# Fifteen pair sums in place of twelve ahead of the transposes of a convolution, with new places for everything around them

## What is computed

```python
enh = _conv(_conv(x, w_conv1_pw, b_conv1_pw, 0), w_conv1_dw, b_conv1_dw, 1, groups=DIM)
h = _conv(x, w_conv2_g, b_conv2_g, 1, groups=INTERC)
h1, h2 = jnp.split(h, 2, axis=1)
attn = _conv(h1 * h2, w_conv2_pw, b_conv2_pw, 0) * attgamma + _conv(x, w_conv211, b_conv211, 0)
# _kba: each pixel has its own 3 x 3 kernel for a pair of channels, a mix of 16 learned sets by attn
bias = jnp.einsum('bpn,nc->bpc', att2, selfb[0])
attk = jnp.einsum('bpn,nm->bpm', att2, selfw[0])
y = jnp.einsum('bpgij,bpgj->bpgi', attk, uf).reshape(Bb, P, C) + bias
x2 = _kba(enh, attn, selfb, selfw) * ga1 + enh
return x2 + x
```

## Time and profile before

| | us |
|---|---|
| median of 3 runs (5731.08 to 5740.74) | 5735.58 |
| profiled execution, its own time | 5731.75 |
| its span | 5730.0 |
| busy TensorE, matmuls / weight loads | 5581.3 (97%) / 4131.5 (72%) |
| busy VectorE | 5083.3 (89%) |
| busy ScalarE | 3463.1 (60%) |
| busy GpSimd | 4185.7 (73%) |
| transposes of terms (L888), by each of the two identities | 6144 matmuls, 920 |
| products (L1100), to the ring / back to PSUM | 1792 of 1.22 / 512 of 1.23 |
| VectorE merges (L1106) | 512 of 1.22 |
| GpSimd merges (L811) | 256 of 2.39 |

### The profile page before, as it was taken

The page is one execution under the profiler, slowest core; times in us unless marked ns, Lnnn a source line. Parts: engine busy times, 40 slices in busy tenths (PEclk is TensorE's granted clock), DMA queues, the critical chain, the costliest instruction groups (busy, mean ns, idle before and its releaser), DMA issues.

```text
span 5730.0 us, 115887 instructions
## 1 busy us (share of the span) xinstructions
PE 5581.3 (97%) x39944; PEld 4131.5 (72%) x39944; DVE 5083.3 (89%) x5319; ACT 3463.1 (60%) x4284; POOL 4185.7 (73%) x1831
## 2 busy tenths in 40 slices
PE   8999999999998699999999999999999999999998
PEld 7888888888886366666666766666666666766666
DVE  7888888888887789999899998989999899998989
ACT  6888888888886455455554555555455554555553
POOL 4565555555654678888888888888888888888885
PEclk9999999999999799999999999999999999999999
DMA  2222222222221222222222222222222222222221
GB/s 89 73 73 73 73 73 77 77 73 73 73 73 62 52 72 67 69 64 65 73 67 70 62 65 71 67 71 66 68 64 65 73 67 70 62 65 71 67 71 45
DMA packets 155248, 394.20 MB, mean 69 GB/s; under 512 B 35136, under 2 KB 38400, under 8 KB 155136
## 3 DMA queue, kind: packets, MB, share of 16 engines
q1 hardware_dynamic: 154800, 392.87, 22.0%
q10 hardware_dynamic: 400, 0.69, 0.1%
HBM read 219.37 MB, written 136.31 MB: 62 GB/s over the span
## 4 chain that ended last, share of the span: by engine, by line
PE 54%; DMA 8%; DVE 3%; SPq 1%; issue 1%; ACT 1%; DVEq 0%; POOLq 0%; POOL 0%; ACTq 0%
PE ps_t L888 18%; PE ps_k L871 17%; DMA xin<-layer_out 8%; PE ps_m L854 8%; PE ps_p L840 5%; PE ps_t L905 2%; DVE products L1100 2%; PE ps_t L896 1%; PE ps_t L903 1%; PE ps_m L861 1%; ACT out_sb L991 1%; SPq L736 1%; DVE products L1062 0%; SPq L684 0%; SPq L711 0%
## 5 line engine op out<-in xcount | busy, mean ns | idle before, releaser
L805 POOL TENSOR_TENSOR enh<-enh,tap 128x1280 f32<-128x1280 f32 (+1 forms) x1024 | 2512.9, 2454 | 485.2 <-ACT tap L1009 431.7
L1100 DVE TENSOR_TENSOR products<-ps_k,enh 128x1024 f32<-128x1024 f32 x1792 | 2157.4, 1221 | 269.4 <-PE ps_k L871 248.5
L871 PE MATMUL ps_k<-att,basis 128*128 128x512 f32 x4608 | 1719.3, 459 | 22.1 <-DVE products L1100 10.9
L1009 ACT ACTIVATE tap<-e,dw 128x1280 f32<-128x1280 f32 (+1 forms) x1024 | 1260.6, 1251 | 0.0
L871 PEld LDWEIGHTS ps_k<-att,basis 128*128 128x128 f32 x4608 | 719.4, 190 | 701.2 <-DVE products L1100 451.1
L296 POOL TENSOR_TENSOR hidden_lo<-hidden,hidden_hi 128x1024 fp32r<-128x1024 f32 x256 | 693.1, 2726 | 717.2 <-DVE hidden_hi L501 717.2
L888 PE MATMUL ps_t<-ident_swap,products 128*128 128x128 f32 x6144 | 921.7, 273 | 0.0
L888 PE MATMUL ps_t<-ident,products 128*128 128x128 f32 x6144 | 919.7, 272 | 0.2 <-POOL products L811 0.2
L888 PEld LDWEIGHTS ps_t<-ident,products 128*128 128x128 f32 x6144 | 757.3, 140 | 175.7 <-POOL products L811 0.5
L811 POOL TENSOR_TENSOR products<-products 128x1024 f32<-128x1024 f32 x256 | 611.8, 2390 | 268.0 <-DVE products L1100 268.0
L888 PEld LDWEIGHTS ps_t<-ident_swap,products 128*128 128x128 f32 x6144 | 719.9, 141 | 0.0
(11 more groups left out here) (111 smaller groups left out, 7378.1 us busy)
## 6 DMA issues: line engine op xcount, KB each, us to landing
xin<-layer_out SPq DMA_DIRECT2D x64, 1280.0 KB, 7.2
xt<-in_x SPq DMA_DIRECT2D x128, 512.0 KB, 4.0
layer_out<-xo SPq DMA_DIRECT2D x128, 512.0 KB, 2.9
x_own<-layer_out SPq DMA_DIRECT2D x128, 512.0 KB, 4.0
out<-out_sb SPq DMA_DIRECT2D x256, 256.0 KB, 2.0
att<-att_hi SPq DMA_DIRECT2D x512, 32.0 KB, 1.9
att<-att_lo SPq DMA_DIRECT2D x512, 32.0 KB, 2.0
h_up<-h_sb SPq DMA_DIRECT2D x256, 16.0 KB
```

The lines of the kernel that those rows point to most:

```text
L805: nc.gpsimd.tensor_tensor(own, own, tap_sb[add % TAP_BUFFERS][:, 0:hi - lo, :], ALU.add).then_inc(dw_done, 1)
L871: mm = nc.tensor.matmul(ps_k[KERNEL_BUFFER[q]][:, BANK * s:BANK * (s + 1)], basis[:, 2 * t + s, :], att[p][:, j, :], start=True, stop=True)
L1009: nc.scalar.activation(tap_sb[add % TAP_BUFFERS][:, 0:hi - lo, :], src, ACT.Copy, scale=dw[:, t:t + 1]).then_inc(tap_ready, 1)
L1100: nc.vector.tensor_tensor(out, kernels, enh[p][:, r:r + CHUNK_ROWS, dx:dx + W].unsqueeze(1).to_broadcast([C, 2, CHUNK_ROWS, W]), ALU.mult) ...
```

## The change

It changes the tables alone. `VECTOR_MERGES` goes from 8 to 10, `POOL_MERGES` from 4 to 5, so a band has 46 ops and slots instead of 44, 21 terms instead of 24, and 26 stored products instead of 28; the ring has 13 places instead of 14, and is gone round twice a band as before. Nearly all the other places are set anew.

```diff
-PRODUCTS = 14
+PRODUCTS = 13
...
-VECTOR_MERGES = (0, 3, 10, 12, 18, 21, 27, 30)
-POOL_MERGES = (6, 15, 24, 33)
+VECTOR_MERGES = (2, 6, 9, 11, 15, 18, 24, 27, 29, 33)
+POOL_MERGES = (0, 4, 13, 21, 31)
...
-TERM_SLOT = {1: 4, 2: 5, 4: 11, 5: 9, 6: 15, 8: 12, 9: 13, 11: 18, 13: 19, 14: 20, 15: 26, 17: 23, 19: 26, 20: 27, 22: 34, 23: 33, 24: 35, 26: 36, 28: 37, 29: 39, 31: 41, 32: 42, 33: 48, 35: 45}
+TERM_SLOT = {0: 11, 3: 6, 4: 16, 7: 11, 8: 10, 10: 13, 12: 18, 13: 23, 16: 23, 17: 24, 19: 26, 20: 30, 21: 33, 23: 31, 25: 33, 26: 35, 28: 39, 30: 45, 31: 47, 34: 44, 35: 48}
...
-BACK_SLOTS = [21, 30, 38, 54]
+BACK_SLOTS = [21, 32, 40, 52]
...
-POOL_MERGE_PLACES = (2.1, 4.5, 10.5, 13.45)
-TAP_PLACES = ((0.6000000000000001, 4.5, 5.0, 9.5, 14.5, 18.0, 18.5, 18.5, 20.5), (23.5, 25.0, 27.0, 30.0, 34.5, 35.5, 36.5, 38.5, 43.0))
-CLEAR_PLACES = (35, 53)
-H_PROD_SLOT = 27
-ATT_HIGH = 29
-ATT_LOW = 32
-CONV_SLOTS = [33, 33, 40, 40, 43, 43, 43, 43, 50, 50, 52, 52, 56, 56, 59, 59, 62, 62]
+POOL_MERGE_PLACES = [0.6000000000000001, 1.6, 4.5, 8.0, 13.9]
+TAP_PLACES = ((0.0, 0.0, 0.0, 1.5, 7.0, 10.0, 12.5, 13.5, 16.0), (22.0, 22.5, 23.0, 26.5, 31.5, 32.5, 35.0, 36.5, 37.5))
+CLEAR_PLACES = [27, 60]
+H_PROD_SLOT = 26
+ATT_HIGH = 26
+ATT_LOW = 35
+CONV_SLOTS = [37, 37, 41, 41, 41, 41, 46, 46, 50, 50, 54, 54, 59, 59, 60, 60, 66, 66]
 COEFFICIENT_SLOT = 28
-PW_SLOTS = [17, 22, 24, 29, 31]
+PW_SLOTS = [17, 19, 25, 30, 36]
```

## The result

The changed kernel takes **5633.0 us** (median of 4 runs, 5629.7 to 5636.0) against 5738.2 (4 runs, 5731.1 to 5741.4): ratio 0.9813, 95% interval 0.9802 to 0.9825, 105 us less. The forecast was 5705, some 30 less. The direction was right and the gain was three and a half times the one forecast. The measured time lies 3 us inside the low end of the range, in what rival 1 called "partly true" (5610 to 5665 us).

What follows compares the result with a forecast made beforehand. Neither TensorE nor VectorE is full; each waits for the other. Period 58.4 to 58.9, middle 58.6, plus 0.15 for h_prod: 58.75 us, 0.52 less, x 62 = 32 us; some 30 off the median gives 5705 us, range 5630 to 5760.

Steps and rivals of the forecast that it cites:

- rival 1: TensorE is the bound and three terms come off whole: 5573 us; partly true, 5610 to 5665 us; together chance 0.22.
- Neither engine full, each waits for the other: In a 59.27 us band VectorE idles 7.1 us and TensorE 1.9, handing two kernel buffers to and fro.
- TensorE's 57.4, VectorE's 52.2 and 54.7: Work in us per band: TensorE 57.4 before, 54.8 after three terms fewer; VectorE 52.2 before, 54.7 after two more merges.
- rival 3: GpSimd and VectorE disturb each other; a GpSimd merge holding VectorE would cost 2.4 us a band, +148 us; chance 0.01.
- the ledger: Slot-by-slot account of TensorE's lateness in a band: 4.9 us of stalls for the new tables, period 58.4 to 59.55 us.
- the room: Slack in the two-buffer handover before TensorE's lateness stalls VectorE: 0.15 us, 0.27 where an op leads into a merge.
- It needs a room of 0.22 instead of 0.15: The slack per op that makes the account of stalls give the old band's 59.27 us; with it the new band is 58.9.
- The latency of 0.86 from one row: Time from the start of a kernel pair on TensorE to its product on VectorE, taken as 0.86 us.
- xin: Pointwise chunk 0's wait for the xin load goes, as the back block moves earlier: between nothing and 0.7 us a band.
- h_prod: VectorE's h_prod, now behind op 26, may wait for h_up: 0 to 0.4 us a band, taken as 0.15.
- a rival of 0.12: h_prod becomes a wait that holds every product behind it; at 1.4 us late the period is 60.0, 5780 us; chance 0.12.
- Pointwise chunk 1, GpSimd, thirteen places, ATT_LOW: Per band, chunk 1 waits 0 to 0.2 us for ScalarE; GpSimd's merges, the smaller ring and ATT_LOW at 35 cost nothing.

Runs made afterwards that it cites:

- run 4: Changed kernel with the GpSimd merge of q 21 undone, so 22 terms instead of 21 and VectorE as before: 5687.1 us.
- run 5: Changed kernel with h_prod computed twice on VectorE, the first time into a buffer nobody reads: 5675.0 us.
- run 10: Kernel before the change with h_prod computed twice on VectorE, first into a buffer nobody reads: 5778.6 us.
- run 1: Kernel before the change with SP issuing the load of xin ahead of the store of chunk 3: 5695.8 us.
- run 2: Changed kernel with the last back block moved from slot 52 to 56: 5695.0 us.
- run 3: Changed kernel with the last back block at slot 56 and xin's load issued ahead of the store of chunk 3: 5670.3 us.
- run 6: Changed kernel with a product's two waits exchanged, first for its ring place, then for its kernels: 5624.5 us.
- run 7: Kernel before the change with a product's two waits exchanged, first for its ring place, then for its kernels: 5727.7 us.
- run 8: Changed kernel with exchanged waits and slots of terms, back blocks, conv taps and pointwise chunks set by the corrected walk; same merges: 5591.1 us.
- run 11: Kernel before the change with a fifth GpSimd merge, of q 13, plus 16 transposes on TensorE ahead of the loop: 5779.5 us.
- run 9: Kernel before the change with a fifth GpSimd merge, of q 13, so 23 terms instead of 24: 6026.1 us.

## Why the prediction was off

**Neither engine full, each waits for the other: right.** Runs 4, 5 and 10 show it. It is also why the busy shares could not choose the side: the conclusion that I drew against the Trainium skill, Perfetto Trace Analysis, Identifying the Most-Contended Engine, stands. By its rule VectorE, at 91% against 69% for the weight loads, was the engine to relieve; the change gave it 2.5 us more work a band and the band got 1.74 shorter. Whether taking work off VectorE would have paid as well was not tried; run 5, where work added to it cost nearly its full price, suggests so.

**TensorE's 57.4, VectorE's 52.2 and 54.7: right as far as the runs tell; 54.8 is 0.3 too high.** The conv taps of slots 59 and 60 fall into slots 13 and 14, and slot 14 has neither kernels nor terms, so the two groups stand next to each other in the queue (the row of 16 matmuls at 3570.20 below). By the prediction's own prices the second costs 0.86, not 1.16. The work is 54.5, TensorE's idle time nearer to 3.0 than 2.7, and some 0.3 us a band of the forecast, 19 us, are this (an estimate). A product still takes 1.22 us with GpSimd at 89%, so rival 3, a disturbance between the two, fell: 1218 ns in the group above, 1221 before.

**The step that failed is the ledger**, "lateness plus the work of the slot less VectorE's step, cut at zero and at the room in each slot that has kernels". It gave 4.9 us of stalls for the new tables and 58.4 to 58.9 a band; the trace has 2.9 and 57.53. The flaw is in the cut: it charges VectorE at slot s with a stall that comes two ops later. The three terms of slots 10 and 11 (cut), then slots 12 to 16 of the changed kernel, TensorE's timeline:

```profile
3565.51 0.60 PE L894 MATMUL ps_t<-ident,products 128*128 128x128 f32 x4
...
3567.70 0.60 PE L894 MATMUL ps_t<-ident_swap,products 128*128 128x128 f32 x4
3568.05 1.34 PE L877 MATMUL ps_k<-att,basis 128*128 128x512 f32 x4
3569.23 0.60 PE L894 MATMUL ps_t<-ident,products 128*128 128x128 f32 x4
3569.67 0.60 PE L894 MATMUL ps_t<-ident_swap,products 128*128 128x128 f32 x4
3570.20 1.94 PE L860 MATMUL ps_m<-xin,gT 128*32 128x512 f32 x16
3572.07 1.20 PE L877 MATMUL ps_k<-att,basis 128*128 128x512 f32 x4
```

and VectorE's, ops 12 to 18 (the last row holds two):

```profile
3566.13 1.22 DVE L1106 TENSOR_TENSOR products<-ps_k,enh 128x1024 f32<-128x1024 f32 x1
3567.38 1.23 DVE L1112 TENSOR_TENSOR products<-ps_k,products 128x1024 f32<-128x1024 f32 x1
3568.80 1.23 DVE L1106 TENSOR_TENSOR ps_k<-ps_k,enh 128x1024 f32<-128x1024 f32 x1 [0.20 <-PE ps_k L877]
3569.95 1.22 DVE L1106 TENSOR_TENSOR products<-ps_k,enh 128x1024 f32<-128x1024 f32 x1
3571.20 1.23 DVE L1112 TENSOR_TENSOR products<-ps_k,products 128x1024 f32<-128x1024 f32 x1
3572.93 2.35 DVE L1106 TENSOR_TENSOR products<-ps_k,enh 128x1024 f32<-128x1024 f32 x2 [0.52 <-PE ps_k L877]
```

Op 12 ends at 3567.35; three terms stand ahead of its kernels, which start at 3568.05, 0.64 late. The ledger takes off the room of 0.27 (a merge follows) and books 0.37 of stall there and then. The merge of op 13 would then end 0.37 later, and the second pair, which by TensorE's own queue could start at about 3568.5 (0.47 on), would wait for it until 3569.0: half a microsecond of idle TensorE, out of which come the term and the conv taps behind it, later by as much. In fact op 13 ran on time and ended at 3568.61, the second pair followed within 0.15 us, and the late pair held up only op 14, by 0.20 to 0.28. A heavy slot is paid for once, two ops on, and the light slot beside it still does its work against the clock that was not yet delayed. Where light and heavy slots alternate, the ledger invents TensorE's idle time (4.8 us; there are 2.7 to 3.0).

The whole band bears it out. In the mean of bands 8 to 60 the changed kernel's VectorE comes late, beyond its own step, by 0.63 us at op 3, 0.16 at op 5, 0.18 at op 11, 0.28 at op 14, 0.60 at op 17, 0.16 at op 20 and 0.27 at op 23. The ledger had its stalls after ops 1, 12, 15, 17, 21 and 36: those after 1, 12, 15 and 21 are found two ops on, at 3, 14, 17 and 23, and there is none of size where those after 17 and 36 would be. The sign was there before the change. The prediction says that the trace has the largest stalls where the ledger has them, after ops 13, 16 and 19. The old trace has three of its four largest at ops 15 (0.93 us), 18 (0.59) and 21 (1.49), and the example in the prediction, product 17 at 3508.32, is op 21.

The corrected walk steps through the ops instead: op a starts at the later of VectorE's own step and the arrival of its kernels, which started at the later of the end of op a - 2 and of what stands ahead in TensorE's queue. It gives 57.48 for the changed kernel, 58.85 for the old one (59.27 measured) and 58.44 without the wait on xin (58.75). It was set up with both traces in hand, so these two are no test of it; and it was adjusted once on the way: for runs 1 to 4 it had 57.51 for the changed kernel, 58.64 for the old one and 58.16 without the wait on xin. For runs 1 to 7 and 10 it had -30, +79, +31, +42, +37, -8, -20 and +37 us (runs 1, 7 and 10 against the kernel before, the others against the changed one); measured were -41, +62, +37, +54, +42, -8.5, -13 and +37. For run 8 it had a band of 56.48, and 56.84 came. Run 11 is its miss: +8 against +40. These differences do not choose between it and the ledger, which had 0 to -25, +40, +40, +50 and +30 for runs 1 to 5 and was nearer than the walk in runs 3, 4 and 8. Against the ledger speak the length of the band itself, the ops at which VectorE is late, and that runs 2 and 3 differ by 25 us where it had them alike.

**"It needs a room of 0.22 instead of 0.15": a warning that I smoothed over.** One number was fitted to the old total and carried over. It absorbed two errors of opposite sign: the cut, and the wait on xin. That the ledger came within 0.4 us of the old band was luck. The room itself is a little smaller by the prediction's own terms: 2.27 - 1.22 - 0.06 - 0.86 is 0.13, not 0.15.

**The latency of 0.86 from one row: half right.** In the rows above the pair at 3568.05 serves op 14 in 0.75 and the pair at 3572.07 serves op 17 in 0.86. Op 14 is the first product of a VectorE merge, which has no place to wait for; op 17 goes to the ring and waits for kernels, then for its place. A merge's first product is 0.1 quicker, and there are ten of these now where there were eight. Runs 6 and 7 show that it is the order of the two waits.

**xin: right in kind, too small.** "The wait goes": it did. Measured alone it was worth 0.52 us a band in the old kernel and 41 us in all. Against the 0.2 to 0.4 of the forecast that is some 16 to 29 us of the 72 between forecast and result, about a third; some 19 are the pair of conv groups, and the rest falls to the ledger's cut.

**h_prod: no wait.** 0.15 was taken and a rival of 0.12 built on it. VectorE's timeline of the changed kernel has it right behind its product, which started at 3583.94:

```profile
3583.94 1.21 DVE L1106 TENSOR_TENSOR products<-ps_k,enh 128x1024 f32<-128x1024 f32 x1
3585.07 0.74 DVE L1126 SCALAR_TENSOR_TENSOR h_prod<-ps_m,bias_h,h_up 128x512 f32<-128x512 f32 x1
3585.72 3.60 DVE L1106 TENSOR_TENSOR products<-ps_k,enh 128x1024 f32<-128x1024 f32 x3
```

In the mean of bands 8 to 60 the step over it is 1.79 us, which is 1.135 and 0.66 and no wait. The last conv group starts at 3578.53, so 6.5 us did. The estimate of 1.5 for h_up's landing was too long, or ScalarE came sooner than "needed" allowed.

**Pointwise chunk 1, GpSimd, thirteen places, ATT_LOW: nothing, as said.** TensorE's idle before chunk 1 (3577.09) shows no wait. GpSimd waits for products (356 us in all), and no term waits for GpSimd. **The last band:** +2 forecast, +4.4 measured.

**What was said would show it:** bands of 58.5 to 59.0 were wanted and 57.53 came, below the 58 at which I had said that the room is wider than I think. It isn't the room that was off, but what was charged against it. VectorE at 96%, the counts of transposes and the end of the wait on xin were as said. TensorE below 97% was not: its row says 99%, as before. That sign could not have shown what it was meant to, since the row said 99% of the kernel before too, with 1.9 us of 59.27 idle by the starts.

Not settled: how the 1.74 us divide between the merges and the new places. Run 1 gives 0.52 for xin; the rest, 1.22, belongs to the merges and the places together (a term more cost 0.83 in run 4, a term less gained nothing in run 11), and no kernel has the new merges with the old places, since the slots themselves are other ones.

## What to carry to other kernels

Where two engines hand two buffers to and fro, work out the start of every operation from its two predecessors, op by op; an account that charged a delay where it arises instead of where it arrives missed most of what this change was worth, and a constant fitted to make it agree with the old total hides that. Neither engine's idle time then hides anything: one instruction of 0.66 us cost 0.6 to 0.7 a band, with 3 and with 7 us of idle time there. Check such an account against the trace op by op, not by its total: here the total agreed and the ops did not. And when a small edit costs far too much, compare the count of code fetches before looking at the schedule.

## What the runs showed of the hardware

- **Where a loop's code lies can cost 4 us a band** (64.08 in run 9, 60.04 in run 11). Run 9 fetched 261 blocks more than the kernel before, and 16 transposes ahead of the loop took them and 247 us away. The Trainium skill, Runtime: NRT & Kernel Launch, Instruction fetch mechanics, gives TensorE an instruction memory of 128 KiB filled in blocks of 16 KiB, and says that the crossing of a block is mostly hidden; it warns that a taken branch out of the window of two blocks forces a fetch and a stall. Such a fetch in every round is not what the kernel before shows, with none between 2170 and 5622 us. Nine fetches a round would fit a loop that touches nine blocks where eight find room. That is argued, not shown: the rows don't say whose code is fetched, only that moving TensorE's put it right and that two of the nine come just ahead of TensorE's stalls. The traces of runs 9 and 11 record 1621 instructions of TensorE in a round. By the 256 instructions that the Trainium skill gives a block there, these are 6.3 blocks (an estimate), so what the others would hold is open. For the two fetches "mostly hidden" does not hold; the other seven leave no stall of such length.
- **The order of two semaphore waits.** 0.77 us from kernels to product with the late semaphore waited for last, 0.86 with it first: some 8 and 13 us of the whole.
- **GpSimd and VectorE side by side.** 1218 ns for a product, of which one operand lies in PSUM, at 89% of GpSimd, 1221 at 82%.
